# Mixture-of-experts stage with gates multiplied into the first layer's output and all nine experts summed in PSUM

## The chip, the cores and the metric

The kernel runs on one core of one Trainium2 chip. Its engines are TensorE (PE: products; its weight loads are listed as PEld), VectorE (DVE), ScalarE (ACT), GpSimd (POOL) and SyncE (SP), which only issues DMAs. The metric is the device time in microseconds, the median of three executions, lower is better. Before the change it is 5180.65 us (5180.65 to 5180.82). The profile is of one further execution.

## The reference, cut to what matters

The program computes four blocks on a 4096 x 128 array x of tokens: a retention block, six layers of local attention with a feed-forward part, a causal attention, and a mixture of experts. Only the last one is touched:

```python
x = x + _L1_ffn_ref(_layernorm(x), ...)          # eps 1e-5
# _L1_ffn_ref(h):   E = 8 experts, H = 512, top 2
var = mean(square(h), -1); normed = h * rsqrt(var + 1e-08) * norm_weight
shared = maximum(normed @ sw1 + sb1, 0) @ sw2 + sb2
probs = sigmoid(normed @ router_w.T)
scores, idx = top_k(probs, 2);  w = scores / (sum(scores) + 1e-06)
comb = zeros((T, E)).at[arange(T)[:, None], idx].add(w)
hdn = maximum(einsum('td,edh->teh', normed, ew1) + eb1, 0)
eo = einsum('teh,eho->teo', hdn, ew2) + eb2
return shared + einsum('teo,te->to', eo, comb)
```

All eight experts are computed for all tokens, and the gates `comb` (zero for the six that a token did not choose) weight them. Everything is fp32.

## The kernel before

Each engine has its own instruction list, written out by hand, and the lists meet only at semaphores. The 4096 tokens are NC = 8 chunks of CH = 512, a chunk is NBLK = 4 blocks of 128. Most arrays are held transposed: 128 features on the partitions, tokens along the free axis (`chunk(buf, c)` is a 128 x 512 piece). PSUM is eight banks `PB[0..7]` of 128 x 512 fp32, listed as D01, D23, D45, D67. TOK is also named XS, RB is XR, RA is EW1, X is EW2; OTb holds the shared weights SW1 and SW2 and two 512-column buffers; XC (two pieces) and V2 hold the hidden layer `HB[0..2]`.

The end of the program goes, in order:

- **Output projection of the attention** (L1484, L1113), whose result x3 stands in XR.
- **Layer norm** (index K_MOE): `norm_tensor` makes the mean with a product (L247) and DVE subtracts it into XC. Then, chunk by chunk: ACT squares, PE makes the variance with four one-column products (L253), DVE adds eps, POOL raises to -1/2 (L304), PE spreads the result over the partitions (L268), DVE multiplies (L286).
- **RMS norm** (index K_RMS), without the mean: the same loop again from XC into XS; ACT then multiplies by the norm weight (L779).
- **Copy of x3 with tokens on the partitions**: 32 PE transposes (L1496) and 8 DVE copies (L1053) into XTOK.
- **Router**: 32 products of 128 x 8 (L1503), a sigmoid on ACT (L781), then the ranking and the gates CM on DVE (L1060 to L1081).
- **Experts**, a hardware loop over the 8 chunks. Per chunk PE transposes the gates (L1513), then for f = 0 (shared) to 8 runs the first layer as four products of 512 columns (L1520), and behind it the second layer of the expert before (`second_layer`, L1125): 16 products of 128 x 128 with the hidden layer as the stationary operand, so that tokens come out on the partitions. The biases of all nine second layers are one 9-row product per block, with the shared expert (L1128). Relu is shared: hidden tiles 0 and 2 on ACT (L790), 1 and 3 on DVE (L1100). DVE's `add_expert` takes each expert from PSUM, multiplies it by its gate, a scalar per token, and adds it to ACC in SBUF (L807; for f = 0 L802 adds XTOK). SP stores each chunk (L445).

Each fp32 product of PE is two MATMUL records and two LDWEIGHTS records in the trace, a transpose is one.

Of the kernel before, what the change touches and what calls it, by code (L numbers as in the profile page):

```python
# [5 lines left out]
def build_program(nc, t, out, scr, xkeep):  # L6
# [4 lines left out]
    ALU = mybir.AluOpType  # L11
# [3 lines left out]
    P = 128  # L15
    D = 128
    BATCH, SEQ = 2, 2048
    CH = 512
# [12 lines left out]
    EPS = 1e-5  # L31
    FF = 341
# [3 lines left out]
    with ctx:  # L36
# [77 lines left out]
        def inner(buf, c):  # L114
# [49 lines left out]
        cmc = sb("cmc", [P, NBLK, NE + 1])  # L164
        cmT = kTb[0:9, 1, 0:CH]
# [7 lines left out]
        CMPB = V2[:, :, :].rearrange("p a n -> p (a n)").rearrange("p (t e j) -> p t e j", e=NE, j=NE)  # L173
        XTOK = OTOK
        ACC = EX.rearrange("p (b n) -> p b n", b=NBLK)
        OUTB = PN.rearrange("p (b n) -> p b n", b=NBLK)
# [18 lines left out]
            "moew_in", "rms_scaled", "xtok_turned", "xtok_copied", "logits", "probs", "rank_gt", "rank_eq", "rank_tri",  # L195
            "rank_sum1", "rank_sum2", "rank", "chosen", "wsum", "winv", "comb",
            "comb_cur", "comb_turned", "comb_copied", "up2", "relu_a", "relu_v", "down2", "acc2", "stored")}
# [40 lines left out]

        block = ctx.enter_context(nc.Block())


        def norm_tensor(pe, k, src, src_sem, src_at, center=True):
            for c in range(NC if center else 0):
# [16 lines left out]
        def spread(pe, k, c):  # L260

            pe.wait_ge(s["rstd_ready"], k * NC + c + 1)
            if c >= 2:
                pe.wait_ge(s["normed"], k * NC + c - 1)
            elif k < K_RMS:
                pe.wait_ge(s["centered"], k * NC + NC - 1 + c)
# [3 lines left out]

        def norm_vector(dve, k, src, dst, after=None, center=True, eps=EPS):
            for c in range(NC if center else 0):
                dve.wait_ge(s["mean_ready"], k * NC + c + 1)
                dve.tensor_tensor(dst(c), src(c), PB[c % 2][:, :], ALU.subtract).then_inc(s["centered"], 1)
            for c in range(NC):
# [3 lines left out]
                dve.tensor_scalar(var_s[:, c % 2, :], PB[2 + c % 2][:, 0:NBLK], eps, None, ALU.add).then_inc(s["var_copied"], 1)  # L279
                if c >= 1:  # L280
                    norm_apply(dve, k, c - 1, src if not center else dst, dst, after)
            norm_apply(dve, k, NC - 1, src if not center else dst, dst, after)

        def norm_apply(dve, k, c, cen, dst, after):
            dve.wait_ge(s["spread_ready"], k * NC + c + 1)
            dve.tensor_tensor(dst(c), cen(c), PB[c % 2][:, :], ALU.mult).then_inc(s["normed"], 1)  # L286
# [3 lines left out]
        def norm_scalar(act, k, dst, ready="centered"):  # L290
            for c in range(NC):
                act.wait_ge(s[ready], (k if ready == "centered" else k - 1) * NC + c + 1)
                if c >= 2:
                    act.wait_ge(s["var_ready"], k * NC + c - 1)
                elif ready == "normed":
                    act.wait_ge(s["var_ready"], k * NC)
# [23 lines left out]
        K_RMS = K_ATT + 2  # L320
# [11 lines left out]
        def _(sp):  # L332
# [48 lines left out]
            for n in range(G):  # L381
# [8 lines left out]
                straddling_windows(n)  # L390
            sp.dma_start(wC[:, :, :], t["wC"]).then_inc(s["w1att_in"], 16)
# [47 lines left out]
            sp.dma_start(mvec[:, :], t["mvec"]).then_inc(s["moew_in"], 16)  # L439
            sp.dma_start(bias2[:, :], t["bias2"]).then_inc(s["moew_in"], 16)  # L440
            sp.dma_start(routw[:, :], t["routw"]).then_inc(s["moew_in"], 16)
            out_v = out.rearrange("(c b p) d -> c p b d", p=P, b=NBLK)
            with sp.Fori(0, NC) as c:
                sp.wait_ge(s["acc2"], c * (NE + 1) + NE + 1 + 3)
                sp.dma_start(out_v[bass.ds(c, 1)].rearrange("a p b d -> (a p) b d"), OUTB).then_inc(s["stored"], 16)  # L445
            sp.wait_ge(s["stored"], 16 * NC + 1)

        @block.gpsimd
        def _(pool):
# [119 lines left out]
            norm_pool(pool, K_RMS)  # L569
# [8 lines left out]
        def _(act):  # L578
# [196 lines left out]
            norm_scalar(act, K_RMS, lambda c: chunk(XC, c), ready="normed")  # L775
            act.wait_ge(s["moew_in"], 16 * 7)
            for c in range(NC):
                act.wait_ge(s["normed"], K_RMS * NC + c + 1)
                act.activation(chunk(XS, c), chunk(XS, c), ACT.Copy, scale=mvec[:, 36:37]).then_inc(s["rms_scaled"], 1)  # L779
# [3 lines left out]
            act.sem_inc(s["relu_a"], 2)  # L783
            with act.Fori(0, NC) as c:
                for f in range(NE + 1):
                    it = c * (NE + 1) + f
                    act.wait_ge(s["down2"], it + 1)
                    for j in (0, 2):
                        act.wait_ge(s["up2"], it * HF + j + 1)
                        act.activation(HB[f % 3][:, j, :], PB[j][:, :], ACT.Relu, bias=mvec[:, f * HF + j:f * HF + j + 1])\  # L790
                           .then_inc(s["relu_a"], 1)

        @block.vector
        def _(dve):
            def add_expert(c, f):

                it = c * (NE + 1) + f
                dve.wait_ge(s["down2"], it + 1 + 3)
                dve.wait_ge(s["acc2"], it + 3)
                yb = PB[4 + f % 3][:, :].rearrange("p (b n) -> p b n", b=NBLK)  # L800
                if f == 0:
                    dve.tensor_tensor(ACC, yb, XTOK[:, bass.ds(c * NBLK, NBLK), :], ALU.add).then_inc(s["acc2"], 1)  # L802
                    return
                if f == NE:
                    dve.wait_ge(s["stored"], 16 * c + 1)
                for b in range(NBLK):
# [814 lines left out]
```

## Time and profile before

| | |
|---|---|
| median of three runs | 5180.65 us |
| profiled execution, its time | 5180.6 us |
| its span, first to last instruction | 5178.8 us |
| PE busy | 4973.2 us, 96% |
| DVE, ACT, POOL busy | 75%, 66%, 52% |
| mean granted TensorE clock | 0.967 |
| instructions | 175419 |

The time is 1.8 us above the span. The page cuts the span into 40 slices of 129.5 us; the mixture of experts with its norms is the last five, from about 4553 us to the end. A chain of waits is read back from the last instruction: each row is the work that released the next, with its start and its length on the path. The granted clock is 1.00 at 2.4 GHz and 0.50 at 1.2 GHz.

### The profile page before, as it was taken

Reading aid. Unit: us, or ns where it says so; the run is one execution under the profiler, and the core shown is the slowest. Engines: PE = TensorE matmul, PEld = TensorE weight load, DVE = VectorE, ACT = ScalarE, POOL = GpSimd, SP = SyncE. Lnnn points to the kernel's source line nnn. Section 1 sums busy time; section 2 is a strip of 40 time slices with the busy share of each in tenths; the row PEclk is TensorE's granted clock in tenths of the full one; section 3 lists DMA queues with packets and bytes.
Section 4 is the critical chain, followed back from the end, with each engine's and each line's share of the span. In section 5 each row is a group of like instructions: output and inputs, shape, how many; then the busy total and the mean of one; then the engine's idle time right before and its main releaser. Section 6 shows DMA issues by size and latency. Waiting matters only on the chain.

```text
span 5178.8 us, 175419 instructions
## 1 busy us (share of the span) xinstructions
PE 4973.2 (96%) x76384; PEld 3261.6 (63%) x76384; DVE 3878.4 (75%) x5096; ACT 3439.4 (66%) x5293; POOL 2705.8 (52%) x1425
## 2 busy tenths in 40 slices
PE   8899999999999999999999999987999999989999
PEld 5577777777777777777777777762333333267677
DVE  5888888888888888888888888836777777443333
ACT  2588888888888888888888877743655566621111
POOL 1877777777777777777777777721111111110000
PEclk8899999999999999999999999977999999979999
DMA  2011111111111112111111111113111111010000
GB/s 75 25 41 47 33 33 44 43 35 34 36 51 35 30 35 56 31 35 34 44 43 35 30 48 34 35 28 74 20 20 20 20 20 20 1 37 4 4 4 4
DMA packets 98013, 168.30 MB, mean 32 GB/s; under 512 B 25081, under 2 KB 36866, under 8 KB 96898
## 3 DMA queue, kind: packets, MB, share of 16 engines
q1 hardware_dynamic: 94402, 148.06, 10.6%
q10 hardware_dynamic: 2880, 9.44, 1.2%
q8 instruction: 588, 9.63, 0.8%
q14 instruction: 143, 1.17, 0.1%
HBM read 47.44 MB, written 10.49 MB: 11 GB/s over the span
## 4 chain that ended last, share of the span: by engine, by line
PE 88%; ACT 3%; issue 2%; DVE 2%; POOL 1%; SPq 1%; DMA 1%; ACTq 0%; DVEq 0%; POOLq 0%
PE D L1333 7%; PE D L1264 7%; PE D L1189 6%; PE D L1275 6%; PE D L1417 5%; PE D L1439 5%; PE D L1292 5%; PE D L1125 5%; PE D L1243 5%; PE D L1520 5%; PE D L1397 4%; PE D L1301 4%; PE D L1170 4%; PE D L1303 4%; PE D L1178 3%; PE D L1205 2%
## 5 line engine op out<-in xcount | busy, mean ns | idle before, releaser
L475 POOL TENSOR_TENSOR rn<-ss,mhalf 128x33 f32<-128x33 f32 (+2 forms) x198 | 1095.8, 5534 | 329.3 <-DVE ss L861 314.8
L1000 DVE TENSOR_REDUCE mxp<-D 128x2 f32<-128x1024 f32 (+3 forms) x640 | 675.6, 1064 | 242.6 <-PE D L1397 130.9
L479 POOL TENSOR_TENSOR hh<-hh,rr 128x1024 f32<-128x1024 f32 x192 | 365.5, 1904 | 405.9 <-DVE rr L913 405.9
L747 ACT ACTIVATE V<-D 128x1024 f32<-128x1024 f32 (+3 forms) x426 | 381.8, 897 | 248.3 <-PE D L1417 242.7
L968 DVE TENSOR_TENSOR TOK<-D,wA 128x1024 f32<-128x1024 f32 x384 | 466.1, 1214 | 0.0
L859 DVE TENSOR_REDUCE ss<-TOK 128x32 f32<-128x2048 f32 x192 | 437.1, 2276 | 0.0
L1333 PE MATMUL D<-PTb,V 64*64 64x32 f32 x24576 | 406.5, 220 | 8.2 <-issue 7.3
L1333 PEld LDWEIGHTS D<-PTb,V 64*64 64x64 f32 x24576 | 381.6, 135 | 34.8 <-issue 10.8
L908 DVE TENSOR_REDUCE rs<-hh 128x16 f32<-128x1024 f32 x192 | 234.2, 1220 | 205.2 <-ACT hh L647 205.2
L675 ACT ACTIVATE V<-D 128x512 f32<-128x512 f32 x384 | 229.6, 598 | 218.9 <-PE D L1301 153.9
L483 POOL TENSOR_TENSOR XC<-XC,TOK 128x1024 f32<-128x1024 f32 x128 | 302.8, 2366 | 46.5 <-DVE TOK L968 46.5
L1243 PE MATMUL D<-RK,w 128*128 128x128 f32 (+1 forms) x2304 | 321.9, 277 | 2.3 <-DVE ss L889 1.4
L964 DVE TENSOR_TENSOR XC<-D,wA 128x1024 f32<-128x1024 f32 x256 | 304.6, 1190 | 8.2 <-ACT TOK L653 7.4
L1316 PEld LDWEIGHTS D<-con,hh 128*128 128x128 f32 x1536 | 161.8, 141 | 230.7 <-issue 151.1
L485 POOL TENSOR_TENSOR XC<-XC,TOK 128x1024 f32<-128x1024 f32 x128 | 302.6, 2364 | 0.0
L747 ACT ACTIVATE hh<-D 128x1024 f32<-128x1024 f32 (+1 forms) x214 | 190.6, 892 | 155.4 <-PE D L1417 154.1
L1292 PE MATMUL D<-kTb,qTb 64*32 64x64 f32 x24576 | 286.5, 225 | 3.3 <-issue 3.2
L1292 PEld LDWEIGHTS D<-kTb,qTb 64*32 64x32 f32 x24576 | 254.7, 105 | 47.6 <-issue 47.5
L1243 PEld LDWEIGHTS D<-RK,w 128*128 128x128 f32 (+1 forms) x2304 | 282.7, 181 | 3.0 <-DVE ss L889 1.5
L613 ACT ACTIVATE OTb<-D 128x1024 f32<-128x1024 f32 x192 | 196.9, 1026 | 131.7 <-PE D L1333 131.7
L655 ACT ACTIVATE TOK<-D 128x1024 f32<-128x1024 f32 x192 | 196.8, 1025 | 131.5 <-PE D L1275 131.5
L1316 PE MATMUL D<-con,hh 128*128 128x128 f32 x1536 | 251.5, 287 | 31.2 <-POOL hh L479 10.3
(241 smaller groups left out, 11689.1 us busy)
## 6 DMA issues: line engine op xcount, KB each, us to landing
V<-V SPq DMA_DIRECT2D x936, 64.0 KB, 2.0
V<-V SPq DMA_DIRECT2D x192, 192.0 KB, 2.5
RB<-watt_dram SPq DMA_DIRECT2D x12, 512.0 KB, 4.2
X<-watt_dram SPq DMA_DIRECT2D x12, 512.0 KB, 3.8
parts_dram<-hh SPq DMA_DIRECT2D x48, 128.0 KB, 2.4
TOK<-parts_dram ACTq DMA_DIRECT2D x36, 128.0 KB
RA<-parts_dram SPq DMA_DIRECT2D x12, 384.0 KB
X<-parts_dram SPq DMA_DIRECT2D x12, 384.0 KB
```

Source lines behind the costliest of these rows:

```text
L475: pool.tensor_tensor(rn[:, st % 2, lo:hi], ss[:, st % 2, lo:hi], mhalf[:, lo:hi], ALU.pow).then_inc(s["powed"], 1)
L479: pool.tensor_tensor(sh, sh, rr[:, :].unsqueeze(2).to_broadcast([P, HEADS, 64]), ALU.mult).then_inc(s["pnorm"], 1)
L747: act.activation(PTE[i % 3][:, 2 * hp:2 * hp + 2, 0:CH - r * P], pair_of(("S", i + LAG, hp))[:, :].rearrange("p (h n) -> p h n", h=2)[:, : ...
L859: dve.tensor_reduce(sums, SQH.rearrange("p (a d) -> p a d", d=DH), AX.X, ALU.add).then_inc(s["reduced"], 1)
L968: return dve.tensor_tensor(swapped.rearrange("p (a q d) -> p a q d", q=2, d=32), src[:, :].rearrange("p (a q d) -> p a q d", q=2, d=32)[:, ...
L1000: dve.tensor_reduce(mxp[:, 2 * hp:2 * hp + 2, qt, kc], pair_of(("F", at, hp))[:, :].rearrange("p (h n) -> p h n", h=2)[:, :, 0:keys], AX.X ...
L1189: m = pe.matmul(D23[:, 0:P], WO[(g // NB) % 2][:, p, :], OTb[:, g % 2, p * P:(p + 1) * P], start=(p == 0), stop=(p == PAIRS - 1))
L1243: m = pe.matmul(D23[0:fn, UP_AT[a][f]:UP_AT[a][f] + P], W1S[(b // NB) % 2][:, a * FF + f0:a * FF + f0 + fn], XAB, start=True, stop=True)
L1264: m = pe.matmul(PB[x], xb, WQ[l % 2][:, x * CH:(x + 1) * CH], start=True, stop=True)
L1292: m = pe.matmul(D45[32 * r:32 * r + 32, at:at + 64], qTb[hs, p * P + 32 * r:p * P + 32 * r + 32], KT[g % 2][hs, p, 32 * r:32 * r + 64], st ...
L1316: m = pe.transpose(D67[:, p * P:(p + 1) * P], SH[g % 2][:, p * P:(p + 1) * P], ident)
L1333: m = pe.matmul(D01[64 * h:64 * h + 64, at:at + WIN], VW[g % 2][ks, (0 if r % 2 else 2) + h, p * DH:(p + 1) * DH], PTb[ks, p * P + 32 * r: ...
```

## The change

Gates are applied before the second layer, not behind it. As relu(h) W2 g = (relu(h) g) W2 for a gate g per token, DVE multiplies the hidden layer of each routed expert in place by its gate (`GB`), and PE then adds all nine experts and the bias product of a chunk in one PSUM bank, `PB[4 + c % 3]`. The second layer now has the weights as stationary operand and 512 tokens as moving one, and its result has features on the partitions. DVE adds x3 once per chunk (`FB`), PE transposes the sum (`turn_out`), ACT copies it out of PSUM and issues the store. XTOK, ACC and `add_expert` go.

The gates must stand on all 128 partitions: PE transposes them (`turn_gates`), ACT copies them to `GT` (nine rows, the ninth ones), SP stores eight rows of 2 KB to DRAM and reads them back, repeated for each partition, in two pieces: experts 1 and 2 (512 KB) and 3 to 8 (1.5 MB).

The order is a list, `EXPERTS`: the shared experts of chunks 0, 1 and 2 come first, since they need no gates; those of chunks 3 to 7 stand behind the third expert of the chunk two earlier. All relus are on ACT. The loops are written out.

The RMS norm is folded into the layer norm: after it the mean square is var / (var + 1e-5), so both factors are one power, (var (1 + 1e-8) + 1e-13)^(-1/2), and DVE multiplies by the norm weight in the same instruction. The load of that weight (`mvec`) comes earlier on SP.

```diff
-        CMPB = V2[:, :, :]...
-        XTOK = OTOK
-        ACC = EX.rearrange("p (b n) -> p b n", b=NBLK)
+        CMPB = V3[:, :, :]...
+        GT = XN[:, :, :].rearrange("p a n -> p (a n)")[0:NE + 1, 0:NC * CH]
+        GB = XL[:, :, :].rearrange("p a n -> p (a n)")[:, 0:NE * CH].rearrange("p (e n) -> p e n", e=NE)
+        FB = [EX, PN]
+        OUTB = [V3[:, x, :] for x in range(2)]
...
+        EXPERTS = [(0, 0), (1, 0), (2, 0)]
+        for ec in range(NC):
+            for ef in range(1, NE + 1):
+                EXPERTS.append((ec, ef))
+                if ef == 3 and 3 <= ec + 2 < NC:
+                    EXPERTS.append((ec + 2, 0))
+        NX = len(EXPERTS)
+        GATES = [(0, 2), (2, NE)]
+        LAST_OF = {ec: n for n, (ec, ef) in enumerate(EXPERTS) if ef == NE}
+        TURN_AT = {2: 0, 4: 1, 5: 2, 6: 3, 7: 4, 8: 5, 9: 6, 10: 7}
+        FIN_AT = {n + 1: ec for ec, n in LAST_OF.items()}
+        OUT_AT = {n + (3 if ec < NC - 1 else 1): ec for ec, n in LAST_OF.items()}
...
# norms
+                    dve.tensor_scalar(var_s[:, c % 2, :], PB[2 + c % 2][:, 0:NBLK], 1.0 + EPS_RMS, EPS * EPS_RMS, ALU.mult, ALU.add)\
...
+                dve.scalar_tensor_tensor(chunk(XS, c), dst(c), mvec[:, 36:37], PB[c % 2][:, :], ALU.mult, ALU.mult)\
-            norm_pool(pool, K_RMS)
-            norm_scalar(act, K_RMS, lambda c: chunk(XC, c), ready="normed")
-            norm_tensor(pe, K_RMS, lambda c: chunk(XC, c), "normed", ...)
...
# SP
+            for c in range(NC):
+                sp.wait_ge(s["comb_copied"], c + 1)
+                sp.dma_start(xkeep[0:NE, c * CH:(c + 1) * CH], GT[0:NE, c * CH:(c + 1) * CH]).then_inc(s["gt_out"], 16)
+                sp.wait_ge(s["gt_out"], 16 * (c + 1))
+                for p, (e0, e1) in enumerate(GATES):
+                    if c:
+                        sp.wait_ge(s["gated_h"], HF * ((c - 1) * NE + e1))
+                    sp.dma_start(GB[:, e0:e1, :], xkeep[e0:e1, c * CH:(c + 1) * CH].unsqueeze(0).to_broadcast([P, e1 - e0, CH]))\
+                      .then_inc(s[f"gate_in{p}"], 16)
...
# ACT, for n in range(NX + 3)
+                    for j in range(HF):
+                        act.wait_ge(s["up2"], n * HF + j + 1)
+                        act.activation(HB[n % 3][:, j, :], PB[j][:, :], ACT.Relu, bias=...)\
+                           .then_inc(s["relu"], 1)
...
+                    act.activation(GT[:, c * CH:(c + 1) * CH], PB[7][0:NE + 1, :], ACT.Copy).then_inc(s["comb_copied"], 1)
...
+                    act.activation(OUTB[c % 2], PB[7][:, :], ACT.Copy).then_inc(s["out_copied"], 1)
...
# DVE, for n in range(NX + 1)
+                    dve.wait_ge(s["gate_in0" if f <= 2 else "gate_in1"], 16 * (c + 1))
+                    for j in range(HF):
+                        dve.wait_ge(s["relu"], n * HF + j + 1)
+                        dve.tensor_tensor(HB[n % 3][:, j, :], HB[n % 3][:, j, :], GB[:, f - 1, :], ALU.mult).then_inc(s["gated_h"], 1)
...
# PE
+            def expert_down(n):
...
+                for k in range(HF):
+                    if f == 0:
+                        pe.wait_ge(s["relu"], n * HF + k + 1)
+                    else:
+                        pe.wait_ge(s["gated_h"], HF * gated_before(n) + k + 1)
+                    m = pe.matmul(PB[4 + c % 3][:, :], w[:, k, :], HB[n % 3][:, k, :], start=(f == 0 and k == 0), stop=False,
+                                  skip_group_check=True)
+                m.then_inc(s["down2"], 1)
+                if f == NE:
+                    pe.wait_ge(s["comb_copied"], c + 1)
+                    pe.matmul(PB[4 + c % 3][:, :], bias2[:, :], GT[:, c * CH:(c + 1) * CH], start=False, stop=True,
+                              skip_group_check=True).then_inc(s["acc_done"], 1)
...
+            pe.wait_ge(s["probs"], 1)
+            for n in range(NX + 3):
+                if n < NX:
+                    expert_up(n)
+                if 1 <= n <= NX:
+                    expert_down(n - 1)
+                if n in TURN_AT:
+                    turn_gates(TURN_AT[n])
+                if n in OUT_AT:
+                    turn_out(OUT_AT[n])
```

How the lists of instructions move is shown at three places. The first is PE between the last spread of a norm and the first expert. Here, before, D01 to D67 are pairs of PSUM banks, `TOK,OTb` is the first layer of the shared expert and `TOK,RA` that of a routed one, ISA and REGISTER_ALU belong to the loop:

```order
L268 MATMUL D01<-con,rstd 128x128 x8
L1496 MATMUL D45<-con,RB 128x128 x32
L1503 MATMUL D67<-routw,TOK 128x8 x32
L1509 UNCONDITIONAL_BRANCH
L1509 ISA
L1511 REGISTER_ALU
L1513 MATMUL D67<-con,cmc 9x128 x4
L1518 ISA
L1520 ISA
L1520 MATMUL D01<-TOK,OTb 128x512 x2
```

And the same place now (L1128 is the first layer, L1141 the second, L1155 the transposes of the gates):

```order
L285 MATMUL D01<-con,rstd 128x128 x8
L1533 MATMUL D67<-routw,TOK 128x8 x32
L1128 MATMUL D01<-TOK,OTb 128x512 x2
L1128 MATMUL D23<-TOK,OTb 128x512 x2
L1128 MATMUL D01<-TOK,OTb 128x512 x2
L1128 MATMUL D23<-TOK,OTb 128x512 x2
L1141 MATMUL D45<-XC,OTb 128x512 x4
L1128 MATMUL D01<-TOK,OTb 128x512 x2
L1128 MATMUL D23<-TOK,OTb 128x512 x2
L1141 MATMUL D45<-XC,OTb 128x512 x4
L1155 MATMUL D67<-con,CM 9x128 x4
L1128 MATMUL D01<-TOK,RA 128x512 x2
```

The L268 before are those of the RMS norm; now the only norm's spread stands right ahead of the router. Three first layers and two second layers of the shared expert now stand between the router and the first instruction that needs the gates (L1155), where before it was the first instruction of the loop.

The second place is PE in the middle of a chunk. Before, the second layer of the shared expert with its biases, and the next:

```order
L1125 MATMUL D45<-OTb,XC 128x128 x4
L1128 MATMUL D45<-bias2,kTb 128x128
L1518 ISA
L1520 MATMUL D01<-TOK,RA 128x512 x2
L1518 REGISTER_ALU
L1520 MATMUL D23<-TOK,RA 128x512 x2
L1117 REGISTER_ALU
L1125 MATMUL D45<-X,XC 128x128 x16
```

Now, the end of one chunk and the transposes of its output (L1166), one and a half experts later:

```order
L1141 MATMUL D67<-XC,X 128x512 x4
L1146 MATMUL D67<-XN,bias2 128x512
L1128 MATMUL D01<-TOK,RA 128x512 x2
L1128 MATMUL D23<-TOK,RA 128x512 x2
L1141 MATMUL D45<-V2,X 128x512 x4
L1128 MATMUL D01<-TOK,RA 128x512 x2
L1128 MATMUL D23<-TOK,RA 128x512 x2
L1141 MATMUL D45<-XC,X 128x512 x4
L1166 MATMUL D67<-con,OTb 128x128 x4
```

Sixteen 128-column products of a second layer became four of 512 columns, the biases one product per chunk in the place of four, and four transposes per chunk are new.

The third place is SP behind the load of the router's weights. Before, the loop with the stores:

```order
L441 DMA routw<-routw_dram 128x8
L443 UNCONDITIONAL_BRANCH
L443 ISA
L445 ISA
L445 DMA out_dram<-OTb 128x4x128
```

Now the round trip of the gates, of which two of eight are shown; the stores of the output stand on ACT:

```order
L463 DMA routw<-routw_dram 128x8
L466 DMA xkeep_dram<-XN 8x512
L471 DMA XL<-xkeep_dram 128x2x512
L471 DMA XL<-xkeep_dram 128x6x512
L466 DMA xkeep_dram<-XN 8x512
L471 DMA XL<-xkeep_dram 128x2x512
```

## Rows read from the trace of the kernel before

**Rows 1.** The page: its first line and PE's busy time.
```profile
span 5178.8 us, 175419 instructions
PE 4973.2 (96%) x76384; PEld 3261.6 (63%) x76384; DVE 3878.4 (75%) x5096; ACT 3439.4 (66%) x5293; POOL 2705.8 (52%) x1425
```
**Rows 2.** Chain of waits, 4800 to 5179 us: shares, then start us, us, what.
```profile
by line: PE D L1125 48.9%; PE D L1520 44.8%; PE D L1128 2.2%; DVE OTb L807 1.4%; PE D L1513 0.8%; issue 0.7%; DVE cmc L1091 0.3%; DVEq L1091 0.1%; DVEq L1088 0.1%; DVEq L805 0.1%; DVEq L36 0.1%
4803.91 3.44 PE D L1520 x8
4807.35 3.57 PE D L1125 x32
4837.85 6.87 PE D L1520 x16
4905.69 6.87 PE D L1520 x16
```
**Rows 3.** Chain of waits, 4560 to 4720 us: second norm to experts.
```profile
4578.13 1.11 PE D L268 x4
4579.25 3.20 PE D L253 x16
...
4599.63 2.58 PE D L1496 x12
...
4605.67 10.62 PE D L1503 x64
...
4616.31 0.39 ACT PR L781
...
4616.73 2.29 DVE hh L1060
...
4632.54 8.65 PE D L1520 x16
...
4642.08 0.41 PE D L1128 x2
4642.49 1.09 PE D L1125 x8
```
**Rows 4.** Windows: length, busy us (count) of PE, PEld, DVE, ACT, POOL; PEclk, DMA.
```profile
4580.00:4590.00 10.00, 10.00 (x50) 10.00 (x51) 2.87 (x8) 2.61 (x5) 4.03 (x4) 0.50 0.00 0
4608.00:4610.00 2.00, 2.00 (x15) 2.00 (x14) 0.00 (x0) 0.00 (x0) 0.00 (x0) 0.67 0.00 0
4610.00:4616.00 6.00, 6.00 (x30) 6.00 (x29) 0.00 (x0) 0.00 (x0) 0.00 (x0) 0.50 0.00 0
4632.00:4636.00 4.00, 4.00 (x8) 1.86 (x7) 0.69 (x2) 0.69 (x1) 0.00 (x0) 0.50 0.00 0
```
**Rows 5.** Chain of waits, 4535 to 4555 us: transposes between 512-column products.
```profile
4547.31 0.44 PE D L1484 x4
```
**Rows 6.** Chain of waits, 4690 to 4712 us: transposes of the gates.
```profile
4701.56 0.60 PE D L1513 x4
```
**Rows 7.** Single lines: duration ns min/median/max, first and last start, form.
```profile
L842 DVE TENSOR_TENSOR XC<-XC,RB x8: 691/693/693, 82.3 to 98.5; 128x512 f32<-128x512 f32 x8
L790 ACT ACTIVATE XC<-D,mvec x96: 687/687/688, 4634.3 to 5159.7; 128x512 f32<-128x512 f32 x96
```
**Rows 8.** DMA issues: queue, count, KB each, median us from issue to landing.
```profile
parts_dram<-hh SPq DMA_DIRECT2D x48, 128.0 KB, 2.4
xkeep_dram<-X SPq DMA_DIRECT2D x1, 2048.0 KB, 13.5
RB<-xkeep_dram SPq DMA_DIRECT2D x4, 512.0 KB, 4.2
```
**Rows 9.** Window in the load of the experts' weights; last number GB/s.
```profile
4544.00:4546.00 2.00, 2.00 (x10) 1.06 (x9) 0.69 (x1) 0.99 (x2) 0.00 (x0) 1.00 1.02 430
```
**Rows 10.** Timeline, 5160 to 5179 us: the last additions and the last store.
```profile
5174.81 1.13 DVE L807 SCALAR_TENSOR_TENSOR OTb<-D,cmc,OTb 128x128 f32<-128x128 f32 x4 [2.54 <-PE D L1125]
5176.10 0.37 SPq L445 DMA_DIRECT2D out_dram<-OTb  x1
```

More of the change, by code:

```diff
@@ L31, in build_program @@
     EPS = 1e-5
+    EPS_RMS = 1e-8
     FF = 341
@@ L269, in spread, with norm_vector @@
             m.then_inc(s["spread_ready"], 1)
-        def norm_vector(dve, k, src, dst, after=None, center=True, eps=EPS):
-            for c in range(NC if center else 0):
+        def norm_vector(dve, k, src, dst, after=None, rms=False):
+            for c in range(NC):
                 dve.wait_ge(s["mean_ready"], k * NC + c + 1)
@@ L438, in _ @@
             sp.dma_start(SW2, t["sw2"]).then_inc(s["moew_in"], 16)
-            sp.dma_start(mvec[:, :], t["mvec"]).then_inc(s["moew_in"], 16)
             sp.dma_start(bias2[:, :], t["bias2"]).then_inc(s["moew_in"], 16)
             sp.dma_start(routw[:, :], t["routw"]).then_inc(s["moew_in"], 16)
[L442 to L446, printed above, removed]
+            for c in range(NC):
+                sp.wait_ge(s["comb_copied"], c + 1)
[6 more added lines that the diff above has]
+                      .then_inc(s[f"gate_in{p}"], 16)
+            for p in range(2):
+                sp.wait_ge(s[f"stored{p}"], 16 * NC // 2)
         @block.gpsimd
@@ L774, in _ @@
             norm_scalar(act, K_MOE, lambda c: chunk(XC, c))
-            norm_scalar(act, K_RMS, lambda c: chunk(XC, c), ready="normed")
[L776 to L779, printed above, removed]
+            act.wait_ge(s["moew_in"], 16 * 6)
             act.wait_ge(s["logits"], 1)
@@ L782, in _ @@
                .then_inc(s["probs"], 1)
[L783 to L791, printed above, removed]
+            out_v = out.rearrange("(c b p) d -> c p b d", p=P, b=NBLK)
@@ L1113, in out_c, with expert_up @@
                 pe.matmul(PB[2 + c % 2][:, :], wC[:, 3, :], chunk(XS, c), start=True, stop=True).then_inc(s["out2"], 1)
[L1115 to L1130 removed]
+            def expert_up(n):
+                c, f = EXPERTS[n]
+                w = SW1 if f == 0 else EW1[:, f - 1, :]
+                for j in range(HF):
+                    if n:
+                        pe.wait_ge(s["relu"], (n - 1) * HF + j + 1)
+                    pe.matmul(PB[j][:, :], w[:, j * P:(j + 1) * P], chunk(XS, c), start=True, stop=True).then_inc(s["up2"], 1)
@@ new lines, in turn_gates, with turn_out @@
+            def turn_gates(c):
+                pe.wait_ge(s["comb"], 1)
+                if c:
+                    pe.wait_ge(s["comb_copied"], c)
+                for b in range(NBLK):
+                    m = pe.transpose(PB[7][0:NE + 1, b * P:(b + 1) * P], CM[:, c * NBLK + b, :], ident)
+                m.then_inc(s["comb_turned"], 1)
+            def turn_out(c):
+                pe.wait_ge(s["fin"], c + 1)
+                if c:
+                    pe.wait_ge(s["out_copied"], c)
+                else:
+                    pe.wait_ge(s["comb_copied"], NC)
+                for b in range(NBLK):
+                    m = pe.transpose(PB[7][:, b * P:(b + 1) * P], FB[c % 2][:, b * P:(b + 1) * P], ident)
+                m.then_inc(s["fin_turned"], 1)
```

158 lines of the change are left out of this document (54 added, 104 removed).

## The prediction

> **What bounds the kernel now.** I read the page first: PE is busy 96% of 5178.8 us [rows 1], so a gain must come off PE's own list or out of the few places where it waits. Then the chain of waits over the experts: 48.9% is the second layer (L1125), 44.8% the first (L1520), and DVE's additions have only 1.4% [rows 2]. A routed expert costs 3.44 us for four 512-column products and 3.57 us for sixteen 128-column ones, 7.01 us together, and a chunk repeats every 4905.69 - 4837.85 = 67.84 us. Nine experts are 63.1 us of that; the other 4.7 us are the bias products and the border of the loop. Third, the chain ahead of the experts [rows 3]: the RMS norm (the L253 from 4579.25 on), the transposes L1496, the router's products L1503, the sigmoid, and then from 4616.73 to 4632.54 no long PE work at all, since DVE ranks the gates and the loop's entry waits. Last the windows for the granted clock: it is 0.50, the 1.2 GHz level, in the norm though PE is busy 10.00 of 10.00 us, and 0.50 in the router's products with 6.00 of 6.00 [rows 4].
>
> **The change part by part.** The sum is made on PE's list, since PE ends the chain everywhere after the change too, if the covers below hold.
>
> *RMS norm folded.* The spread that starts at 4578.13 ends 1.11 us later, at 4579.24. The router's products follow at once; the second pass (4579.25 to 4599.63, 20.4 us) and the 32 transposes L1496 (4599.63 to 4605.67, 6.0 us) are gone with their DVE copies and ACT's scaling. DVE's multiplication gets the norm weight as a scalar in the same instruction. PE is never idle in that stretch at 1.2 GHz [rows 4], so a slightly longer DVE step is hidden; even 0.1 us in each of eight steps on the path would be 0.8 us. The norm weight is loaded a whole attention block earlier, one more DMA on SP ahead of the weights wC: nothing.
>
> *Router.* L1503 took 10.62 us [rows 3]. The clock fell from 1.00 to 0.50 on the way: the window 4608 to 4610 shows 0.67, so x + (2 - x)/2 = 1.34 gives x = 0.68 us, the fall is at 4608.68, and 3.01 us ran at 2.4 GHz. The clock had risen during the transposes L1496. These are gone, and the norm ran at 0.50 throughout, so I let the whole router run at 0.50: 10.62 + 3.01 = 13.63 us, to 4592.87. The other end is the whole at 2.4 GHz, 13.63 / 2 = 6.8 us. The sigmoid adds 0.39 and two semaphores: the first expert starts at 4593.3 instead of 4632.54, 39.2 us earlier.
>
> *Ranking.* With the loop's entry and the gates' transposes it lay between 4616.73 and 4632.54, at most 15.8 us; from 4593.3 that ends by 4609.1. PE now has three first layers and two second layers of the shared expert first, 5 x 3.44 = 17.2 us plus the slow clock of 1.8 us (below), and asks for the gates at 4612.3. The ranking is hidden, with 3 us to spare.
>
> *Second layer with 512 columns.* Same form and count of records as the first layer, so 3.44 us for 3.57. Two first layers in a row take 6.87 us [rows 2]; 72 experts at that are 494.6 us. The bounds for a second layer that accumulates 36 products in one bank, which no row shows: 3.44 and 3.57. I take 3.44, as the operands have the first layer's shape; the other end costs 72 x 0.13 = 9.4 us.
>
> *Biases.* The 9-row products took 0.41 us for two records and made the next eight L1125 1.09 instead of 8 x 3.57 / 32 = 0.89 [rows 3]: 0.19 us more on each side of a change of shape. One product of 512 columns is 3.44 / 4 = 0.86, so 0.86 + 0.38 = 1.24 us, eight times 9.9 us. From below: 0.86 each, 3 us less.
>
> *Transposes.* Four in a row between longer products take 0.44 us [rows 5], four for the gates 0.60 behind a wait [rows 6]. Eight sets for the gates and seven for outputs stand in the stream: 15 x 0.44 = 6.6 us, by 0.60 it would be 9.0.
>
> *Clock at the first expert.* Before, the first sixteen records took 8.65 us for 6.87, because the clock was still 0.50 until 4636 [rows 3, 4]. The same 1.8 us again.
>
> *Covers.* ACT has four relus of 0.687 per expert, DVE four multiplications of 0.693 [rows 7], 2.8 us each against PE's 6.87. The first layer's results are needed 3.44 us later, behind another expert's second layer, so relu plus gate (1.4 us) never reaches PE. ACT waits at the output for PE's transposes, with the next relus behind it; these come due only with PE's next first layer. DVE's additions and the copy of the gates at the border of a chunk, for which PE stood still for over 1 us, are gone. Two instructions wait for DMAs: DVE's first multiplication, with all later ones and PE's second layers behind it. For chunk 0: gates transposed by 4612.7, ACT's copy 0.7, store 2.4, read 4.2 [rows 8], semaphores 0.2, first multiplication 0.7: 4620.9. PE wants it after two first layers and one second, 4612.7 + 10.3 = 4623.0. Hidden, with 2 us to spare; the read repeats rows of DRAM, which no row shows. Later chunks have far more time (below).
>
> *Sum.* Experts 494.6 + 9.9 + 6.6 + 1.8 = 512.9 us, from 4593.3 to 5106.2; before, PE ended a semaphore (0.12 us) ahead of DVE's last addition of 5174.81 [rows 10], so 4632.54 to 5174.69 = 542.2. The end was 4.1 us, 5174.69 to 5178.8. Now: semaphore 0.12, DVE's addition 0.69, transposes 0.60, ACT's copy 0.69, three hand-overs 0.25, and the store from issue to end 5178.8 - 5176.10 = 2.7 [rows 10]: 5.05 us. The span becomes 5111.3 us, 67.5 us less: 39.2 + 29.3 - 1.0. The profiled execution took 5180.6 us for 5178.8, so 5113.1 us; its time is 0.05 us under the median of the runs.
>
> **A rule against the rows.** The granted clock was 0.50 in 4580 to 4590 with PE and its weight loads busy 10.00 of 10.00 us [rows 4]. The Trainium skill (TensorE: Matmul & The Clock Gate, section Why this matters for your kernels) says that a TensorE kept busy continuously gets into its full clock. By the row the router takes 13.6 us, by the rule 6.8 and no slow start of the experts. The trace does not agree for these short products, which have one or eight columns behind a full weight load. The Trainium skill (DMA: Bandwidth & Descriptors, section Anatomy of one DMA) gives about 2.0 us plus bytes over 436 GB/s per DMA, an estimate of 5.6 us for the 1.5 MB piece; it would leave the sum as it is and speaks against the last rival.
>
> **Rivals.**
>
> *The clock rises during the router or at its end* (what the rule above says): 6.8 us less for the router and up to 1.8 for the first expert, 5113.1 - 6.8 to 8.6 = 5104.5 to 5106.3. For it: L1496, also short, was accompanied by a rise. Against it: the clock fell while L1503 ran, and the same norm ran at 0.50 for over 30 us.
>
> *The first gates come late.* If the store or the read take 3 to 7 us longer than above, PE waits once in chunk 0, 1 to 5 us: 5114 to 5118. For it: a store and a read in series with 2 us to spare; the 2 MB store into the same tensor took 13.5 us [rows 8]. Against it: this store is 16 KB.
>
> *The second layer gains nothing from 512 columns*, 3.57 us: 5113.1 + 9.4 = 5122.5. Against it: L1520's row, the same form.
>
> *The repeated read of the gates becomes the bound, and the kernel slower.* The 1.5 MB of chunk c may start only when expert 8 of chunk c - 1 has been multiplied, and expert 3 of chunk c must have it: 3 x 6.87 us further, plus 5.4 us by which DVE runs ahead of PE, 26 us. Beyond that PE waits in each of seven chunks. The gain of 67.5 is used up at 67.5 / 7 = 9.6 us more, a read of 35.7 us, 44 GB/s; at 40 us per read the time would be 5113.1 + 7 x 14 = 5211. For it: 128 partitions read the same 12 KB of DRAM, no row has that. Against it: reads of DRAM in pieces of 2 KB ran at 430 GB/s [rows 9], ten times as fast.
>
> **How the numbers follow.** The forecast 0.67, the clock 0.10, late gates 0.11, no gain by columns 0.07, the read as bound with a slower kernel 0.03, and 0.02 for the read taking away just the gain. Likeliest 5113.1 us. Its own terms leave 3 us below (biases) and 2.4 above (transposes at 0.60); the range goes on down to the clock's case, 5105, and up to no gain by columns, 5123. About 0.2% (10 us) is what the measurement can tell from no change: faster 0.95, within 0.2% 0.02, slower 0.03.
>
> **What would show it.** Right: no second run of variance products; the first expert's product some 0.4 us behind the last router product, near 4593; second layers of 3.44 us for eight records; PE without idle time from there to the end, a chunk every 64 us; DVE and ACT under 45% busy beside it; clock 0.50 in the router, 1.00 some 3 to 4 us into the experts. Wrong: PE waiting in a second layer for DVE's multiplication, with a DMA behind that (late gates in chunk 0, the read as bound in all); a router of 7 us (clock); second layers of 3.57 us. A stall at the output's transposes or at ACT's store would be something I have not seen.

## The result, and the profile after

| | before | changed |
|---|---|---|
| median (range) of four runs | 5180.65 us (5176.67 to 5180.82) | 5114.19 us (5113.25 to 5120.2) |
| ratio, 95% interval | | 0.9876, 0.9863 to 0.9889 |
| profiled execution, its time | 5180.6 us | 5113.65 us |
| its span | 5178.8 us | 5111.9 us |
| start of the last spread of the norm | 4578.13 | 4577.77 |
| from there to the end of the span | 600.7 us | 534.1 us |

By the medians the kernel is 66.5 us faster, by the ratio of the runs 1.24% (1.11% to 1.37%). The last line is the part that the change touches, 66.6 us shorter. I use it below, since the stages ahead of it vary from one execution to the next.

The page of the changed kernel, its first line and the busy times; they answer to [rows 1]:

```profile
span 5111.9 us, 170786 instructions
PE 4924.5 (96%) x74512; PEld 3078.3 (60%) x74512; DVE 3856.5 (75%) x4912; ACT 3539.8 (69%) x5437; POOL 2699.3 (53%) x1417
```

The pages cover the whole program, so the part behind the last spread has windows of its own (length, busy us and count of PE, PEld, DVE, ACT, POOL, granted clock, DMA share, GB/s), first before, then changed:

```profile
4578.13:5178.80 600.67, 568.35 (x3172) 417.84 (x3172) 219.14 (x461) 109.60 (x160) 8.56 (x17) 0.96 0.01 4
```

```profile
4577.77:5111.90 534.13, 528.13 (x1300) 241.22 (x1300) 196.39 (x277) 208.52 (x306) 0.46 (x9) 0.98 0.18 36
```

PE has 40.2 us less work there, and its idle time falls from 32.3 to 6.0 us. So 26 us of the gain was idle time of PE, which the busy share of 96% on both pages doesn't show. The larger part is the stretch of the ranking; the other is the border of a chunk, where PE waited for DVE in the kernel before (engine, line, releaser: us, times, longest):

```profile
PE D L1513 <- DVE cmc L1091: 12.2, 7, 1.7
```

The chain of waits of the changed kernel, from the last spread into the experts (start us, us on the path, what); L285 is now the spread, L1533 the router, L804 the sigmoid, L1128 the first layer, L1141 the second, L1155 the gates' transposes. It answers to [rows 3]:

```profile
4577.77 1.11 PE D L285 x4
4578.89 13.47 PE D L1533 x64
4592.42 1.28 ACT L804
4593.72 0.39 ACT PR L804
...
4594.15 9.00 PE D L1128 x16
4603.15 3.43 PE D L1141 x8
...
4613.45 0.44 PE D L1155 x4
```

The second pass and the transposes L1496 are gone, and the router stands right behind the norm. Between it and the sigmoid is a row that the prediction doesn't have, 1.28 us of ACT without an output. The timeline names it. Of the changed kernel:

```profile
4592.42 1.28 ACT L804 ACT_TABLE_LOAD   x1 [20.17 <-PE D L1533]
```

And of before:

```profile
4601.13 1.28 ACT L781 ACT_TABLE_LOAD   x1
```

Before, ACT loaded its table for the sigmoid while PE was still at the transposes L1496, which last until 4605.67 [rows 3]; now the load starts when the router is done.

The windows of the changed kernel, in the same form, answer to [rows 4]:

```profile
4580.00:4590.00 10.00, 10.00 (x48) 10.00 (x49) 0.00 (x0) 0.00 (x0) 0.00 (x0) 0.50 0.00 0
...
4594.00:4598.00 4.00, 3.85 (x5) 1.78 (x6) 3.87 (x2) 0.81 (x3) 0.00 (x0) 0.51 0.01 4
4598.00:4602.00 4.00, 4.00 (x10) 1.74 (x10) 3.96 (x3) 3.25 (x5) 0.00 (x0) 1.00 0.00 0
...
4620.00:4630.00 10.00, 10.00 (x27) 4.47 (x26) 4.91 (x8) 4.21 (x7) 0.00 (x0) 1.00 0.93 162
...
4640.00:4700.00 60.00, 60.00 (x158) 26.85 (x157) 20.32 (x30) 25.42 (x38) 0.00 (x0) 1.00 0.20 40
```

The router runs at 0.50 throughout, the clock rises some 4 us into the experts, and from then on PE is busy in every microsecond with DVE at 20.32 and ACT at 25.42 of 60 us. The DMA share of 0.93 at 4620 is the repeated read of the gates.

The chain in the middle and at the end, with the bias product L1146 and DVE's last addition L1110, answers to [rows 2, 10]:

```profile
4738.82 3.43 PE D L1141 x8
4742.25 1.05 PE D L1146 x2
4743.30 3.63 PE D L1128 x8
...
4805.74 1.05 PE D L1146 x2
...
5107.10 0.70 DVE OTb L1110
```

A second layer takes 3.43 us where it took 3.57 [rows 2], and a chunk 4805.74 - 4742.25 = 63.49 us where it took 67.84.

Read off the two chains, the 66.6 us are: 20.4 for the second pass and 6.0 for L1496, less 2.9 for a router that now runs wholly at 0.50, 14.5 between the router and the first expert (16.3 before, 1.8 now), 29.2 in the experts, less 0.7 at the end. The 29.2 in turn are some 10 us for the second layers' columns and, by my estimate from the same chains, 9 for the bias products (2.4 us a chunk before, 1.25 now) and 9 to 10 for the borders of the chunks. Of these three only the columns have a run of their own (cols128).

### The profile page after: what moved, and what is told of

It reads as the page before. It is cut to its first block, busy times and chain, and to the rows that moved or that the text cites. A ratio compares the mean times of both kernels' runs of the same rounds, so it can differ in the third digit from the quotient of the medians.

```text
span 5111.9 us, 170786 instructions
## 1 busy us (share of the span) xinstructions
PE 4924.5 (96%) x74512; PEld 3078.3 (60%) x74512; DVE 3856.5 (75%) x4912; ACT 3539.8 (69%) x5437; POOL 2699.3 (53%) x1417
## 3 DMA queue, kind: packets, MB, share of 16 engines
HBM read 64.22 MB, written 10.62 MB: 15 GB/s over the span
## 4 chain that ended last, share of the span: by engine, by line
PE 89%; ACT 3%; issue 2%; DVE 2%; POOL 1%; SPq 1%; DMA 1%; ACTq 0%; POOLq 0%; DVEq 0%
PE D L1370 7%; PE D L1301 7%; PE D L1226 7%; PE D L1312 6%; PE D L1454 5%; PE D L1476 5%; PE D L1329 5%; PE D L1280 5%; PE D L1128 5%; PE D L1141 5%; PE D L1434 4%; PE D L1338 4%; PE D L1207 4%; PE D L1340 4%; PE D L1215 3%; PE D L1242 2%
## 5 line engine op out<-in xcount | busy, mean ns | idle before, releaser
L1104 DVE TENSOR_TENSOR XC<-XC,XL 128x512 f32<-128x512 f32 x184 | 126.7, 692 | 218.0 <-ACT XC L814 202.3
## 6 DMA issues: line engine op xcount, KB each, us to landing
XL<-xkeep_dram SPq DMA_DIRECT2D x8, 1536.0 KB, 11.5
```

## The experiments

The stages ahead ended between 4565.82 and 4579.83 us in the profiled executions (start of the last spread), and on one chip the kernel before ran from 5168.56 to 5193.98 us. A difference of 10 us between medians can be that alone, so each kernel is read by its own ratio and by the time from the last spread to the end of the span, called the tail. The kernels of one group ran on one chip.

| kernel | group | median us | ratio to before, 95% interval | tail us |
|---|---|---|---|---|
| before | | 5180.65 | | 600.7 |
| changed | | 5114.19 | 0.9876 (0.9863 to 0.9889) | 534.1 |
| fold_only | 1 | 5160.35 | 0.9963 (0.9953 to 0.9974) | 582.6 |
| in_order | 1 | 5123.94 | 0.9891 (0.9872 to 0.991) | 544.05 |
| cols128 | 1 | 5126.64 | 0.9898 (0.9879 to 0.9917) | 544.3 |
| table_early | 1 | 5106.24 | 0.9854 (0.9835 to 0.9874) | 533.55 |
| read_x2 | 2 | 5113.12, one run | | 534.3 |
| read_x3 | 2 | 5181.73 | 1.0005 (0.9993 to 1.0017) | 604.45 |
| read_distinct | 2 | 5112.29, one run | | 534.1 |
| mix | 2 | 5110.73 | 0.9877 (0.986 to 0.9895) | 536.5 |
| after_again | 3 | 5108.55 | 0.986 (0.9842 to 0.9877) | 534.0 |
| table_again | 3 | 5109.72 | 0.9864 (0.9845 to 0.9884) | 533.6 |
| blocks | 3 | 5114.06 | 0.9866 (0.9846 to 0.9887) | 536.7 |

### fold_only: the kernel before with the folded norm alone

```diff
- norm_pool(pool, K_RMS)
- norm_scalar(act, K_RMS, lambda c: chunk(XC, c), ready="normed")
- norm_tensor(pe, K_RMS, ...)      # and DVE's part, and ACT's product with the norm weight
+ # DVE, last step of the one norm that is left
+ dve.scalar_tensor_tensor(chunk(XS, c), dst(c), mvec[:, 36:37], PB[c % 2][:, :], ALU.mult, ALU.mult)
```

> The kernel before with the RMS norm folded into the layer norm, and nothing else of the change (gates, order and loops as before). My sum: the second pass of 20.4 us goes; if the sigmoid's table load (1.28 us in the changed kernel) is again behind the router's last product, 1.3 us come back on the path: 19.1 us less, 5161.5 us. Rival 1 (the pass costs more than its own time, since it also scaled on ACT and kept DVE busy): over 22 us less, under 5158.6. Rival 2 (the table load is hidden as before): 20.4 us less, 5160.2, and the profile has it before the router's end.

The tail is 600.7 - 582.6 = 18.1 us shorter, where I had put it at 19.1. Rows of its chain:

```profile
4580.42 11.07 PE D L1503 x64
...
4609.08 9.21 PE D L1520 x16
```

The pass is worth 20.4 us [rows 3]. Of that, 1.3 go to the table load, which in this kernel too comes behind the router. The router gives back 11.07 - 10.62 = 0.45 and the first expert 9.21 - 8.65 = 0.56, and 20.4 - 1.3 - 0.45 - 0.56 = 18.1. So the table load on the path belongs to the fold, not to the new order of the experts. It does not come of the transposes L1496, which this kernel still has: before, ACT's scaling by the norm weight stood between its wait for the weights and its wait for the router, and with the scaling gone both waits stand in front of the sigmoid (see table_early). That the slower clock in router and first expert is a cost of the fold isn't shown by one trace; the first expert's row alone went from 8.80 to 9.16 us in profiles of the changed kernel and of those that leave this place as it is. The other 48.5 us of the change come of all that is not the fold: transposes, ranking's cover, experts.

### in_order: every expert in its own chunk

```diff
-        EXPERTS = [(0, 0), (1, 0), (2, 0)]
-        for ec in range(NC):
-            ...
-        TURN_AT = {2: 0, 4: 1, ...}
+        EXPERTS = [(ec, ef) for ec in range(NC) for ef in range(NE + 1)]
+        TURN_AT = {0: 0, 4: 1, ...}
```

> The changed kernel with the experts in plain order, chunk by chunk with the shared one first, and the gates of chunk 0 transposed behind the first shared first layer. My theory: the three shared experts only cover the ranking of the gates, 13.7 us from the sigmoid. PE then has 5.6 us of work and waits 8.1 us for the gates; the round trip of the gates stays hidden behind two first layers and a second; with up to 2 us for a clock that falls again: 8 to 10.5 us slower than the changed kernel, 5122 to 5124.7 us. Rival (the round trip through DRAM is what the order hides): PE waits in the second layer of expert 1 as well, 14 us or more slower, 5128 or above. Rival (the order is worth nothing): 5114.

The tail is 9.95 us longer than the changed kernel's. A row of its waits (engine, line, releaser: us, times, longest), and two of its chain; L1150 are the transposes of the gates, L1123 the first layer:

```profile
PE D L1150 <- DVE CM L1090: 8.2, 1, 8.2
```

```profile
4609.21 1.02 PE D L1150 x4
4610.23 4.77 PE D L1123 x8
```

PE waits 8.2 us for the ranking, and after the wait the clock is down again: 1.02 us for transposes of 0.44, and 4.77 for a first layer of 3.43, together 1.9 us. That is the 9.95 within 0.2. So the shared experts of three chunks ahead are what hides the ranking. PE has no wait for the gates' way through DRAM here, so the rival that the order hides this round trip falls.

### cols128: the second layer in 128-column products

```diff
-                    m = pe.matmul(PB[4 + c % 3][:, :], w[:, k, :], HB[n % 3][:, k, :], ...)
+                    for b in range(NBLK):
+                        cols = slice(b * P, (b + 1) * P)
+                        m = pe.matmul(PB[4 + c % 3][:, cols], w[:, k, :], HB[n % 3][:, k, cols], ...)
```

> The changed kernel with each second layer as sixteen products of 128 columns again, the weights still stationary and the sums still in one PSUM bank. My theory: the columns per product alone make 3.57 us of 3.43, 0.14 us for 72 experts: 9.8 us slower, 5124 us. Rival (the 3.57 us came of the hidden layer as stationary operand, or of its blocks): second layers stay at 3.43 and the time at 5114.

The weights stay the stationary operand and the sum stays in one bank; only the length of a product is that of before. Its chain:

```profile
4600.58 3.57 PE D L1143 x32
```

That is the 3.57 us of [rows 2] again, and the tail grows by 10.2 us, 0.14 for each of 72 layers. So the columns alone make this part of the gain, not the other operand as weights and not the one bank. The rival of no gain falls.

### table_early and table_again: the table load back under the router

```diff
-            norm_scalar(act, K_MOE, lambda c: chunk(XC, c))
             act.wait_ge(s["moew_in"], 16 * 6)
+            norm_scalar(act, K_MOE, lambda c: chunk(XC, c))
```

> The changed kernel with ACT's wait for the experts' weights moved ahead of the norm's squares, so that the sigmoid has one wait only. My theory: in the changed kernel two waits stand ahead of the sigmoid, the router's lands on the table load, and its 1.28 us come onto the path; here the load is done during the router: 1.3 us faster than the changed kernel, 5112.9 us, the first expert starting 0.4 us behind the last router product. Rival: the load happens late for another reason: no change, 5114.2, the load still behind the router.

In the changed kernel two waits stand ahead of the sigmoid, for its weights and for the router. Here the first is met already in front of the norm, so that one is left. The rows are those of its second run, table_again; the timeline shows the load, the chain what followed:

```profile
4574.33 1.28 ACT L804 ACT_TABLE_LOAD   x1
```

```profile
4594.44 0.39 ACT PR L804
...
4594.87 9.75 PE D L1128 x16
```

The load is hidden, 1.3 us. But the first sixteen records take 9.75 where they took 9.00 us: what starts earlier has the slow clock for longer. The clock rises 20.2 us behind the last spread in the changed kernel (window 4597 to 4598 at 0.53) and 20.3 in this one (4600 to 4601 at 0.91). The tail is 0.55 us shorter, not 1.3. The median of 5106.24 us looked like 8 us gained; 5.7 of them are that the last spread started at 4572.05. To settle it, the same kernel and the changed one, without an edit, ran once more on one chip:

> The changed kernel itself, beside the next two on the same chip, as the size to which their times are compared; executions of one kernel differed by up to 18 us in the last runs, all of it ahead of the norm. Expected: 5105 to 5120 us, and 534 us from the last spread of the norm (L285 x4) to the end, as in its first profile (5111.9 - 4577.8).

> table_early once more, beside the changed kernel on the same chip. My theory (only the table load's 1.28 us differ, and the stages ahead decide the rest by chance): 532.8 to 533.6 us from the last spread to the end, time 0 to 2 us under after_again. Rival (the first run's 5106 us was the change's own doing): again 6 to 8 us faster.

The tails are 534.0 and 533.6 us, the medians 5108.55 and 5109.72, the ratios 0.986 and 0.9864. In the medians table_again is 1.2 us over and not under. The 0.4 to 0.6 us in the traces stand on the path in both pairs and are far below what the medians can tell.

### read_x2 and read_x3: the 1.5 MB read two and three times

```diff
+        REPS = 3      # 2 in read_x2
...
+                    for rep in range(REPS - 1 if p and c else 0):
+                        sp.dma_start(GB[:, e0:e1, :], xkeep[e0:e1, ...]...to_broadcast(...)).then_inc(s["gate_rep"], 16)
+                        sp.wait_ge(s["gate_rep"], 16 * ((c - 1) * (REPS - 1) + rep + 1))
```

> The changed kernel with the 1.5 MB read of gates done twice in a row for chunks 1 to 7, the second behind the first. One such read took 11.5 us in the changed kernel. My theory (26 us between the last multiplication of a chunk and the moment at which PE needs expert 3 of the next): 23.5 us are hidden, no change, 5114 us, PE without waits. Rival (the reserve is only the 20.6 us of three experts, DVE's lead does not count): 2.9 us per chunk, 20 us slower, 5134.

One read takes 11.5 us in the changed kernel (queue, count, KB each, median us from issue to landing; the 512 KB one 5.0):

```profile
XL<-xkeep_dram SPq DMA_DIRECT2D x8, 1536.0 KB, 11.5
XL<-xkeep_dram SPq DMA_DIRECT2D x8, 512.0 KB, 5.0
```

Twice that is 23 us, and the tail stays at 534.3 us, with no wait of PE for the gates.

> The same with three reads in a row, 35.5 us. My theory: 9.5 us of waiting in each of seven chunks, 66 us, and up to 2 us more each time if the clock falls in the wait: 5180 to 5194 us, that is no faster than the kernel before, with PE waiting in the second layer of expert 3 for DVE. Rival (the reads of this kind are hidden whatever they take, since they run beside PE): 5114.

Three in a row are 34.5 us, beyond the 26 us that the prediction gave as reserve. One chunk's border in the chain, with L1146 the second layer here, the same layer one chunk on, and the waits:

```profile
4677.18 11.42 DMA XL<-xkeep_dram
...
4700.44 0.70 DVE XC L1109
...
4701.19 5.09 PE D L1146 x8
...
4773.78 6.34 PE D L1146 x8
```

```profile
PE D L1146 <- DVE XC L1109: 51.7, 7, 8.2
```

PE waits in each of seven chunks, 7.4 us on average, behind DVE's multiplication and that behind the DMA. The whole gain is gone: ratio 1.0005 (0.9993 to 1.0017). The prediction put this point at 35.7 us per read. Reads of 34.5 us reach it, because the wait also costs clock: the layer after it takes 5.09 us for 3.43 the first time and 6.34, 6.71, 5.55, 6.65, 5.79 and 6.33 us the six other times. That is 18.4 us more, and with the 51.7 us of waiting it makes 70.1 of the 70.3 us. By waits of 7.4 us for 34.5 us of reading the reserve is some 27 us.

### read_distinct: as many bytes, no row read twice

```diff
-                    sp.dma_start(GB[:, e0:e1, :], xkeep[e0:e1, c * CH:(c + 1) * CH].unsqueeze(0).to_broadcast([P, e1 - e0, CH]))
+                    sp.dma_start(GB[:, e0:e1, :], t["ew1"].rearrange("e p n -> p e n")[:, e0:e1, :])
```

It leaves the gates out: weights of the first layer are read in their place.

> The changed kernel with the multipliers read from 128 different places of DRAM (the experts' first weights) instead of one row repeated 128 times; sizes, pieces of 2 KB and waits are the same. It leaves the gates out of the hidden layer. My theory: the repetition of the same 12 KB makes the read slow (11.5 us for 1.5 MB, 163 GB/s in its window); distinct rows land in 4 to 6 us. Rival (pieces of 2 KB into this buffer are slow whatever their source): 11.5 us again. No change in time either way, 5114 us, as the reads are hidden.

```profile
XL<-ew_dram SPq DMA_DIRECT2D x8, 1536.0 KB, 7.2
```

Same size, same destination, 7.2 us for 11.5, the 512 KB one 3.5 for 5.0. I had put it at 4 to 6. A window in this kernel's read shows it too:

```profile
4616.00:4620.00 4.00, 4.00 (x10) 1.71 (x9) 1.74 (x3) 0.67 (x1) 0.00 (x0) 1.00 0.91 322
```

The DMA engines are busy in both, share 0.91 at 322 GB/s here and 0.93 at 162 in the changed kernel's window 4620 to 4630 (above). So the source alone makes the difference. Most likely it is that all 128 partitions read the same rows, but the source here is also another tensor, and one that was not stored just before; this run doesn't tell these apart. For the repetition speaks that 512 KB read without it from the same tensor, xkeep, took 4.2 us [rows 8]. The tail is 534.1 us in both kernels, so it costs nothing here.

### mix and blocks: what raises the clock

Both put first layers into the router's stretch, to have the 2.4 GHz sooner. mix puts one 512-column product each ahead of the router's products of chunks 2 to 5, blocks a whole first layer ahead of those of chunks 2 and 5:

```diff
# mix
+                if 2 <= c < 6:
+                    ...
+                    pe.matmul(PB[c - 2][:, :], SW1[:, (c - 2) * P:(c - 1) * P], chunk(XS, 0), ...).then_inc(s["up2"], 1)
# blocks
+                if c == 2:
+                    ...
+                    expert_up(0)
+                if c == 5:
+                    expert_up(1)
```

Both also have the earlier wait of table_early and leave out PE's wait for the sigmoid (`pe.wait_ge(s["probs"], 1)`) ahead of the experts.

> The changed kernel with the four products of the first shared first layer set between the router's products (behind chunks 2 to 5 in turn), and the wait of table_early. My theory of the clock: it stays at 0.50 in norm and router because the short products behind full weight loads do not raise it, and 512-column products among them do. Then the router runs mostly at 1.00: its end some 1 to 3 us earlier than without although 3.4 us of other work are in it, the first expert's slow stretch is gone: with the table load 5 to 8 us faster than the changed kernel, 5106 to 5109 us. Rival (the clock needs an unbroken stretch of long products): router and first layer together at 0.50, 20 us, no gain beyond the table load, 5112.5 to 5114.

A window of mix and its chain (L1541 router, L1536 the single products, L1131 the next first layer):

```profile
4574.00:4594.00 20.00, 20.00 (x73) 15.87 (x71) 0.75 (x1) 4.03 (x5) 0.00 (x0) 0.50 0.00 1
```

```profile
4574.24 3.21 PE D L1541 x16
4577.46 1.91 PE D L1536 x2
...
4594.52 6.31 PE D L1131 x8
```

My theory fell: the clock stays 0.50 for the whole 20 us, the router and the first layer take 20.3 us as the rival said, and the next first layer still starts at 0.50, 6.31 us for 3.43. The tail is 2.4 us longer.

> The changed kernel with the first layers of the first two shared experts each as one unbroken block of four 512-column products among the router's, behind chunks 1 and 4, and the wait of table_early. In mix single products between short ones left the clock at 0.50. My theory (an unbroken block raises it, and it stays up for some 3 us of short products behind, as it did behind the transposes L1496 before the change): six of eight chunks of the router at or near 1.00, 3 to 5 us less from the last spread to the end than after_again, 529 to 531 us. PE then waits up to 4 us for the ranking, since 3.4 us of its cover stand ahead of the sigmoid. Rival (a block of 3.4 to 6.9 us is too short among such products, the clock stays at 0.50): 536 to 540 us, since the router ends later and the cover is gone.

The chain of blocks (L1543 router, L1132 first layer, L1159 the gates' transposes) and its wait:

```profile
4578.71 3.21 PE D L1543 x16
4581.93 6.46 PE D L1132 x8
4588.39 2.58 PE D L1543 x24
4590.96 5.23 PE D L1132 x8
4596.19 2.59 PE D L1543 x24
...
4612.93 1.02 PE D L1159 x4
4613.95 5.71 PE D L1132 x8
```

```profile
PE D L1159 <- DVE CM L1099: 3.8, 1, 3.8
```

Here the clock rises towards the end of the unbroken block (window 4587 to 4588 at 0.66), and 24 router records take 2.58 us where the changed kernel's rate of 13.47 / 64 gives 5.05. It falls right behind them (4591 to 4592 at 0.55; 5.23 us for eight records of 3.43) and rises again within the second block, so that the last 24 take 2.59. Six of eight chunks of the router run at 1.00, as I had forecast. The stretch gets shorter, but two of the first layers that hid the ranking now run ahead of it: PE waits 3.8 us for the gates, the clock falls (2.9 us more in the last two rows than at full clock), and the tail is 536.7 us for the 529 to 531 forecast. The wait was in that sum; not in it were the two blocks, which themselves run partly at 0.50 (6.46 and 5.23 us for 3.43), and the slow clock behind the wait. That the router runs at 1.00 behind unbroken blocks and not among single products holds, the gain doesn't come. What in a block raises the clock, the two kernels don't tell. None of these kernels beats the changed one by more than can be measured.

One more thing can be read from both: in the changed kernel PE waits 1.8 us for the sigmoid, though the first layers behind it use nothing of its result, and the transposes of the gates wait for the ranking anyway. A kernel that drops this wait alone was not run. By table_early, where a start 1.3 us earlier brought 0.55, I estimate less than 1.8 us for it.

## Why the prediction was right, step by step

The forecast was 5113.1 us, the profiled execution took 5113.65 and the median is 5114.19. It rests on several terms, of which some were off in opposite directions.

*RMS norm folded.* Right: no second run of products, 20.4 and 6.0 us gone; fold_only has the first alone. One term was missed, the table load of 1.28 us, which the sum puts at nothing. With ACT's scaling gone, a second wait stands ahead of the sigmoid and the load comes onto the path. The lost transposes are not the reason: fold_only still has them and shows the load behind the router, and table_early hides it without them.

*Router at 0.50.* 13.47 us for 13.63, clock 0.50 throughout. The rival of a rising clock falls, and mix holds the clock at 0.50 even with four long products between. The Trainium skill (TensorE: Matmul & The Clock Gate, section Why this matters for your kernels) has a TensorE that is kept busy continuously reach its full clock. The trace agrees for the experts' 512-column products (1.00 from 4598 on) and not for the router's, 13.47 us without a pause at 0.50.

*Start of the first expert.* 4594.15 for 4593.3: 1.30 us of load, less 0.36 by which the stages ahead ended earlier, and 0.16 from the router.

*Ranking.* Hidden, as said, with 5.7 us to spare for the 3 forecast: the gates are done at 4607.8, and PE asks for them at 4613.45. in_order shows the price without the cover, 9.95 us; in blocks two of the three first layers stand ahead of the sigmoid, and PE waits 3.8 us.

*Experts.* From 4594.15 to 5107.07, 512.9 us, as forecast. Inside, each layer has 3.43 for 3.44 (0.4 us in all), the bias product costs 1.05 and 0.20 in the next layer, 1.25 for 1.24, the transposes 0.44. The first sixteen records took 9.00 us where 8.67 were assumed. The waits are 1.8 us before the experts and 0.8 at the last output, none between:

```profile
PE D L1128 <- ACT PR L804: 1.8, 1, 1.8
...
PE D L1166 <- DVE OTb L1110: 0.8, 1, 0.8
```

*First gates.* The timeline of the round trip:

```profile
4614.54 0.29 SPq L466 DMA_DIRECT2D xkeep_dram<-XN  x1
4616.01 0.89 SPq L471 DMA_DIRECT2D XL<-xkeep_dram  x2
4621.75 4.91 DVE L1104 TENSOR_TENSOR XC<-XC,XL 128x512 f32<-128x512 f32 x8 [13.97 <-DMA XL<-xkeep_dram]
4624.03 3.60 PE L1141 MATMUL D<-XC,X 128*128 128x512 f32 x8
```

Store to the issue of the read 1.5 us for 2.4, the read 5.7 for 4.2: the two errors cancel but for 0.6 us. The first multiplication ends at 4622.4, and PE reaches for it at 4624.2, 1.8 us to spare for the 2 forecast. The rival of late gates stayed a rival by that much.

*The read as bound.* The reserve of 26 us was right within about 1 us (read_x2, read_x3). The price was low: each wait also cost 1.7 to 3.3 us of clock behind it, which the rival left out. The duration of one read was not known and is 11.5 us. The estimate of 5.6 us is not borne out; read_distinct with 7.2 us is nearer to it. The figures that it is worked out from stand in the Trainium skill (DMA: Bandwidth & Descriptors, section Anatomy of one DMA) as a fit for DMAs issued from GpSimd, and these reads are issued from SP.

*End.* 4.83 us for 5.05.

The sum over all: -0.36 upstream, -0.16 router, +1.30 load, 0.0 experts, -0.22 end, +0.6 us of span. The steps hold but for the missing table load, which smaller errors of the other sign made up for in part. The closeness of half a microsecond is chance, since the stages ahead alone move the time by more than that.

## What to carry to other kernels

When a stage is removed, list what ran unseen beside it (a table load, a read, a ranking) and which waits now stand together, and not only what waited for it; the table load took 1.3 us of the fold's 20.4 for that reason. Price a wait on TensorE with the slower products behind it: waits of 4 to 8 us here cost another 1.7 to 3.3 us each. Compare variants that touch only the end of a program from a fixed point of the trace on, where stages ahead drift by more than the difference in question.

## What the runs showed of the hardware

- A read in which 128 partitions take the same 12 KB of DRAM moved 162 GB/s with the DMA share at 0.93; as many bytes from distinct rows of another tensor moved 322 at 0.91.
- With two waits ahead of an activation that needs a new table, the later wait held up the load too, 1.28 us on the path (fold_only and the changed kernel); with one wait the load ran ahead, 15 us before the sigmoid in the kernel before and 20 us in table_again (4574.33).
- PE with weight loads was busy 20.00 of 20.00 us at 0.50 in mix, with single 512-column products among the router's. In blocks the clock rose within an unbroken eight-record first layer, stayed at 1.00 for the 2.58 us of the 24 short records behind it, and fell at the start of the next first layer (4591 to 4592 at 0.55).
